# Attention scores from rounded parts in two passes, projections one iteration earlier, row moves split, new orders

## The reference, cut to what matters

```
def _gqa(x, wq, wk, wv, wo):            # 16 heads of 16, 4 key/value heads
    q = (x @ wq.T).reshape(B, S, 16, 16)
    k = (x @ wk.T).reshape(B, S, 4, 16)   # v the same, k and v repeated 4 times
    attn = jnp.einsum('bqhd,bkhd->bhqk', q, k) * scale
    attn = softmax(where(causal, attn, -inf))
    return jnp.einsum('bhqk,bkhd->bqhd', attn, v).reshape(B, S, C) @ wo.T
```

## Time and profile before

| what | us |
|---|---|
| median of 3 runs (2116.47 to 2120.29) | 2118.55 |
| the profiled execution | 2111.37 |
| its span, first to last instruction | 2109.7 |
| busy: TensorE / VectorE / ScalarE / GpSimd | 2036.1 / 1347.3 / 1117.4 / 963.0 |

### The profile page before, as it was taken

How to read it: one execution, slowest core, us unless ns; L and a number is a source line. 1 busy time by engine, 2 the same in 40 slices (tenths; PEclk the granted TensorE clock), 3 DMA queues, 4 the chain that set the end, 5 groups by cost and what they waited for, 6 DMA issues and landing times. The chain is left out here.

```text
span 2109.7 us, 50236 instructions
## 1 busy us (share of the span) xinstructions
PE 2036.1 (97%) x17544; PEld 1752.2 (83%) x17544; DVE 1347.3 (64%) x2818; ACT 1117.4 (53%) x2219; POOL 963.0 (46%) x1062
## 2 busy tenths in 40 slices
PE   7999989999999999989979999999899999999997
PEld 7999985666666666659979999999888888888886
DVE  7888954676777767765636776788654444444452
ACT  6777744666666666655543333344354444454542
POOL 0000002365565556556644444444245656565653
PEclk9999987999999999989989999999999999999998
DMA  8767711133233232229864444544344444545442
GB/s 294 264 260 267 261 59 31 62 104 96 92 108 110 87 106 96 78 92 305 300 218 144 148 151 142 175 150 151 104 96 109 95 111 95 112 96 111 96 83 30
DMA packets 134682, 289.62 MB, mean 137 GB/s; under 512 B 23026, under 2 KB 64755, under 8 KB 128243
## 3 DMA queue, kind: packets, MB, share of 16 engines
q1 hardware_dynamic: 84466, 177.25, 24.9%
q0 software_dynamic: 50048, 110.14, 20.3%
HBM read 187.17 MB, written 95.42 MB: 134 GB/s over the span
## 5 line engine op out<-in xcount | busy, mean ns | idle before, releaser
L1248 DVE TENSOR_REDUCE neg_max<-ring 128x2 f32<-128x512 f32 (+1 forms) x384 | 250.0, 681 | 106.4 <-PE ring L1734 106.1
L1041 POOL TENSOR_SCALAR_AFFINE_SELECT weights_diag<-weights_diag 128x512 f32<-128x512 f32 x256 | 158.3, 643 | 258.4 <-ACT weights_diag L1139 258.1
L2908 POOL DMA_INDIRECT out<-q_t,row_put x128 | 201.8, 1576 | 162.4 <-ACT q_t L2972 137.7
L3046 DVE TENSOR_TENSOR ex_hid<-ex_up_ps,gelu 128x512 f32<-128x512 f32 x128 | 86.9, 688 | 171.8 <-ACT gelu L2956 171.8
L2956 ACT ACTIVATE gelu<-ex_gate_ps 128x512 f32<-128x512 f32 x128 | 76.3, 596 | 187.3 <-PE ex_up_ps L62 187.3
L2379 POOL DMA_INDIRECT picked_rows<-results,lo_row_now x128 | 134.0, 1047 | 56.3 <-issue 29.8
L1139 ACT ACTIVATE weights_diag<-ring 128x512 f32<-128x512 f32 x256 | 138.5, 599 | 24.2 <-PE ring L1752 24.2
L60 PE MATMUL ex_down_ps<-ex_dn_lo,ex_hid_hi 128*128 128x256 f32 x512 | 145.1, 283 | 2.8 <-issue 2.8
L61 PE MATMUL ex_down_ps<-ex_dn_hi,ex_hid_lo 128*128 128x256 f32 x512 | 145.2, 284 | 0.0
L62 PE MATMUL ex_down_ps<-ex_dn_hi,ex_hid_hi 128*128 128x256 f32 x512 | 144.9, 283 | 0.0
L1049 POOL DMA_INDIRECT sorted_rows<-h_sb,row_now x128 | 126.8, 990 | 34.8 <-issue 31.3
(11 more groups left out here) (404 smaller groups left out, 7521.8 us busy)
## 6 DMA issues: line engine op xcount, KB each, us to landing
ug_raw<-in_w_ug SPq DMA_DIRECT2D x32, 1028.0 KB, 5.0
dn_raw<-in_w_dn SPq DMA_DIRECT2D x32, 640.0 KB, 5.2
q_t<-sorted_rows SPq DMA_DIRECT2D x136, 128.0 KB
moe_w<-in_expert_gu SPq DMA_DIRECT2D x16, 1024.0 KB, 4.8
results<-c0n POOLq DMA_DIRECT2D x33, 256.0 KB, 4.4
x_raw<-in_x_t SPq DMA_DIRECT2D x32, 256.0 KB, 5.1
c0n<-c SPq DMA_DIRECT2D x32, 256.0 KB, 4.3
c0r<-c SPq DMA_DIRECT2D x32, 256.0 KB
```

Of the source, the lines that this page charges most:

```text
L1041: nc.gpsimd.affine_select(part, part, [[0, G], [1, P]], ALU.is_ge, 0.0, base=0, channel_multiplier=-1).then_inc(kept_done, 1)
L1248: nc.vector.tensor_reduce(out, src, AX_X, ALU.max, negate=True).then_inc(max_done, 1)
L2908: nc.gpsimd.indirect_dma_start(out=out_rows, out_offset=bass.IndirectOffsetOnAxis(ap=at, axis=0), in_=eo[c][:, n, :], in_offset=None, comp ...
L3046: nc.vector.tensor_tensor(hid[f % 2][:], up_ps[f % 2][:], gelu[f % 2][:], ALU.mult).then_inc(hid_done, 1)
```

## The change

It does the following.

- Queries and keys are kept as rounded parts. `q_t` is [128, 2, 4, 256] fp32r: index 0 the high parts; index 1, for even heads, their low parts in one half of a group's 32 rows and high parts in the other (for odd heads the halves swapped). `k_t` becomes three tiles: the high keys with two rows of ones behind them, and two with high keys in one half of the rows and low keys in the other. The key projection gives the keys twice, in both halves.
- A score is two fp32r matmuls: high by high (16 rows), then both mixed products at once (32 rows). A turned score is one of 512 columns with 18 rows, then two of 256 columns (even and odd heads).
- The maximum is split in two rounded parts (`split_max`), so its transpose has 32 columns and its shift is moved by two DMAs.
- New work: ACT `keep_k` (two activations of 256 columns) and `copy_low` (512); DVE `low_q` (512) and two scalar_tensor_tensor for the keys in place of one tensor_scalar; SP 4 moves (`move_high`) in the iteration of the projection and 8 (`move_beside_low`) in the next, in place of 4.
- Maxima and exponentials take two banks at once (6 instead of 12 of each per sequence).
- Projections are for sequence i+3, square sums for i+4; the loop starts at iteration -2.
- **TensorE's order after:** turned 0, turn_max 0, project_out, scores 0, turn_norm, values 1, turned 1, turn_h, heads 0, scores 1, heads 1, keys_values, turned 2, queries 0 and 1, turn_max 1, scores 2, prefix, gate, turn_out, values 0. In B_ORDER shift_q1 comes before route.
- Buffers of other stages serve as q_t, k_t, and in the expert stage other tiles as `eo`. One wait of SP in the sort (`s == 6`) is dropped.

```diff
@@ turned_scores (PE)
                 for g in range(NKV):
-                    rows = slice(32 * g, 32 * g + HD + 1)
-                    nc.tensor.matmul(slot(2 * r, g)[:], k_t[n][rows, k * P:(k + 1) * P], q_t[n][rows, :, q * P:(q + 1) * P],
-                                     start=True, stop=True).then_inc(turned_done[g], 1)
+                    rows = slice(32 * g, 32 * g + HD + 2)
+                    nc.tensor.matmul(slot(2 * r, g), k_t[n][0][rows, keys], q_t[n][rows, 0, :, toks], start=True, stop=False)
+                for odd in range(2):
+                    for g in range(NKV):
+                        rows = slice(32 * g, 32 * g + HALF)
+                        out = slot(2 * r, g).rearrange("p (j s) -> p j s", j=G)[:, odd:G:2, :]
+                        last = nc.tensor.matmul(out, k_t[n][1 + odd][rows, keys], q_t[n][rows, 1, odd:G:2, toks], start=False, stop=(odd == 1))
@@ scores (PE)
-                    for g in range(NKV):
-                        rows = slice(32 * g, 32 * g + HD)
-                        if r and c == 0 and g >= 2:
-                            until(pe, exp_done, no_more_than(times(12, i, 4 * r + g - 1), 12 * B))
+                    for rest in range(2):
+                        for g in range(NKV):
+                            rows = slice(32 * g, 32 * g + (HALF if rest else HD))
+                            if r and c == 0 and not rest and g == 2:
+                                until(pe, exp_done, no_more_than(times(12, i, 4 * r + 2), 12 * B))
@@ Front
+    def keep_k(self, act, b, k_t):
+        self.nc.scalar.activation(k_t[1], self.piece_b[:, 0:S], ACT.Copy).then_inc(self.k_hi_done, 1)
+        self.nc.scalar.activation(k_t[0], self.piece_b[:, 0:S], ACT.Identity, bias=rows[:, 0:1], scale=rows[:, 1:2]).then_inc(self.k_hi_done, 1)
     def keep_kv(self, dve, b, k_t, v):
-        self.nc.vector.tensor_scalar(k_t[:], self.piece_b[:, 0:S], self.at.one_rows[:], None, ALU.add)
+        dve.wait_ge(self.k_hi_done, 2 * b + 2)
...
+        self.nc.vector.scalar_tensor_tensor(out=k_t[2], in0=high, scalar=rows[:, 3:4], in1=self.piece_b[:, 0:S], op0=ALU.mult, op1=ALU.add).then_inc(self.k_odd_done, 1)
+        dve.wait_ge(self.k_odd_done, b + 1)
+        self.nc.vector.scalar_tensor_tensor(out=k_t[1], in0=high, scalar=rows[:, 2:3], in1=self.piece_b[:, 0:S], op0=ALU.mult, op1=ALU.add).then_inc(self.b_free, 1)
+    def low_q(self, dve, b, q_t):
+        dve.wait_ge(self.q_hi_done, b + 1)
+        self.nc.vector.tensor_tensor(q_t[:, 1, 0:G:2, :], self.piece_a[:].rearrange("p (j s) -> p j s", j=QB), q_t[:, 0, 0:G:2, :].bitcast(F32), ALU.subtract).then_inc(self.a_free, 1)
+    def copy_low(self, act, q_t):
+        self.nc.scalar.activation(q_t[:, 1, 1:G:2, :], q_t[:, 1, 0:G:2, :].bitcast(F32), ACT.Copy).then_inc(self.q_lo_done, 1)
@@ split_max (DVE)
+                dve.wait_ge(max_done, times(12, b, 8 if q else 12))
+                nc.vector.tensor_tensor(max_parts[q][:, 0, :], whole, nothing[:, 0, 0:1].broadcast_to([P, NH]), ALU.add).then_inc(max_hi_done, 1)
+                dve.wait_ge(max_hi_done, times(2, b, 1 if q else 2))
+                nc.vector.tensor_tensor(max_parts[q][:, 1, :], whole, max_parts[q][:, 0, :].bitcast(F32), ALU.subtract).then_inc(max_parts_done[q], 1)
@@ body (SP)
+                if exists(later(i, 2)):
+                    front.move_beside_low(sp, i[1] + 2, q_t[(i[1] + 2) % 4])
                 if exists(later(i, 1)):
                     move_shift(later(i, 1), 1)
-                if exists(later(i, 2)):
-                    move_odd_heads(i)
+                if exists(later(i, 3)):
+                    front.move_high(sp, i[1] + 3, q_t[(i[1] + 3) % 4])
```

302 lines of the change are left out of this document (162 added, 140 removed).

## The result

Slower: 2150.38 us (median of 4 runs, 2146.24 to 2157.73) against 2119.26 (2116.47 to 2120.29) for the kernel before on the same chip, a ratio of 1.0153 with a 95% interval of [1.012, 1.0186]. The prediction was 2100, range 2070 to 2130: wrong in sign and outside the range. The profiled execution after took 2153.45 us with a span of 2151.8, that of before 2111.37 with 2109.7: the two traces differ by 42.1 us, of which the medians show 31.

A forecast was written before the change was run, and what follows sets the result against it. TensorE's own work in program order was taken to bound the attention stage. 28 iterations x (18.6 - 19.43) = -23.2, with +4 and +0.5 giving -18.7: 2092.7 us against the profiled execution, 2100 against the median, range 2070 to 2130.

The forecast's parts named there:

- TensorE's part: Attention stage: shorter turned and score bursts, none gained in round 2, save 2.15 us an iteration, 19.43 becoming 17.28.
- Rival 3: Rounded bursts in row groups bound by their weight loads, over 0.95 us each: slower, 2134 to 2147 us; chance 0.12.
- (a): Queries wait for divide(1), now behind round 1's second-pair reduction: stall 0.35 us in odd iterations, 1.1 in even ones.
- (b): Between gate and turn_out: turn_out waits for the piece keep_logits frees, behind a two-bank reduction of round 2; stall 0.55 us.
- the part on VectorE: VectorE's work grows by net 1.4 to 15.1 us an iteration, binding only by order; with stalls, iterations average 18.6 us.
- stall (c): Score bursts of rounds 1 and 2 wait after two groups for a two-bank exponential: 0.1 us in round 1.
- SP's queue: Moves and shifts fill 11.2 of 18.6 us an iteration; no queue is full, and the shift lands with margin 0.8 at worst.
- rival 4: Shift of the maximum lands late behind eight more moves, 1 us in each iteration: 2120 to 2127 us; chance 0.06.
- Rival 2: VectorE late throughout even iterations (turn_max, out_low, key parts wait), 19.3 us: about 2115 to 2128 us; chance 0.14.
- The sign of being wrong: Listed signs against the forecast: bursts of over 0.9 us, or an iteration under 18.0 or over 19.2 us.
- Start and end: Around the attention loop: first turned score 6.5 us later, 2.5 credited at the end; net +4 us, between 0 and +10.

The follow-up runs named there:

- run 14: Changed kernel with rows to scatter early on VectorE and GpSimd's first pair of scatters between the halves of its triangles: 2118.7 us, ratio 1.0021.
- 5: Changed kernel with VectorE's rows to scatter and four index searches put back ahead of the first maxima of scores round 0: 2153.8 us, ratio 1.0182.
- 7: Run 5 with extra, unread matmuls in two TensorE waits (ahead of the queries; between gate and turned output): 2142.3 us, ratio 1.0123.
- 15: Run 14 with extra, unread matmuls in TensorE's two waits: 2108.2 us, ratio 0.997.
- run 2: Changed kernel with the gate (and prefix) back between the two halves of the queries on TensorE: 2211.3 us, ratio 1.043.
- 9: Changed kernel with exponentials and maxima one bank at a time again, as before the change: 2145.1 us, ratio 1.0129.
- run 12: Run 10 with extra, unread matmuls in two TensorE waits: 2236.4 us, ratio 1.0562.
- 13: Changed kernel without the second pass of the turned scores (8 matmuls fewer in each of three bursts): 2112.1 us, ratio 1.0004.
- 16: Kernel before the change with GpSimd's four scatters of an iteration at the end of its order: 2118.1 us, ratio 1.0024.
- run 18: Run 15 with two instead of three extra matmuls between gate and turned output: 2128.1 us, ratio 1.0055.
- run 1: Changed kernel without the eight moves of rows beside the low parts: 2136.6 us, ratio 1.0089.
- 4: Kernel before the change with eight more moves an iteration, into a tile nothing reads: 2122.0 us, ratio 1.0017.
- 3: Changed kernel with divide(1) put back ahead of the maxima of scores round 1's second half on VectorE: 2163.7 us, ratio 1.021.
- 8: Run 5 with the gate between the turned maxima and scores round 2, logits kept ahead of round 2's maxima: 2156.3 us, ratio 1.0183.
- 10: Changed kernel with GpSimd's four scatters of an iteration at the end of its order: 2235.7 us, ratio 1.0558.

## Why the prediction was wrong

**TensorE's part** held, with one term off. Turned bursts 0.68 us (forecast 0.64), scores of round 0 0.59 (0.54), of round 2 0.95 (0.88). Round 1 takes 0.73 even where nothing waits (run 14, 693.44 to 694.17), and was put at 0.54 like round 0. Savings by these: 3 x 0.39 + 0.38 + 0.24 + 0.05 = 1.84 us instead of 2.15, so 17.6 us of work and not 17.3. VectorE's and ScalarE's work came as forecast too: 363.36 and 321.88 us of 500, 15.1 and 13.3 us an iteration (15.1 and 13.4). Rival 3 did not come: a rounded burst takes 0.59 to 0.95 us. The Trainium skill ("TensorE: Matmul & The Clock Gate", section "The mechanism") states that a load overlaps running matmuls only where the row group differs. With 0.11 us for a load and as much for a stream (an estimate from the earlier trace rows), the score burst of round 0 would then take 4 x 0.22 = 0.88. It takes 0.59, so the trace disagrees.

**Stalls (a) and (b)** came in their place: (b) with 12.0 / 24 = 0.50 us a wait, (a) smaller than forecast, 11.0 us over 24 iterations, 0.46 (0.35 and 1.1, mean 0.7). That (b) agrees with its 0.55 is in part luck: its terms, 0.1 + 1.21 + 0.2 + 0.07, make 1.58, and against 8 x 0.11 = 0.88 they leave 0.70.

**The step that failed** is the sum of an iteration at the end of the part on VectorE: "Odd iterations: 17.2 + 1.0 = 18.2; even: 17.4 + 1.75 = 19.1". An iteration took 20.71 us. The sum took it to be work plus stalls at full clock, so the clock has no term in it, and stall (c), "0.1 in round 1", took the exponential to start as soon as TensorE's burst ends.

First, the clock. The prediction used, with its 1.00, for the time after the change as well, although its own forecast put a microsecond or more of waiting into every iteration of an engine that had none. The granted 0.95 over 500 us is 50 us at the lower level; where TensorE works all through them they cost 25 us, about 1.0 us an iteration. Filling the waits, with TensorE doing more, gave 11.5 us (5 to 7) and 10.5 us (14 to 15), which is net of the filling. That the waits let the clock fall and that this costs time is shown; which waits do it is not. Less idle time went with a lower clock in runs 2 and 9, and the filling of run 12 left it at 0.89.

Second, the late posts: 11.9 us of waits in scores, 0.5 us an iteration where (c) had 0.1, and 2.6 in heads, where the prediction had none; together 0.6 us an iteration. Moving the scatters (with the rows early) gave some 28 us (14), leaving out the second pass of the turned scores some 32 us, 20 of them for its work (13). In both the late posts are gone, but the clock stays at 0.94, so it does not hang on them alone. No row of the kernel before could show the late posts: its bursts don't provoke them, neither with the scatters across a turned score (719.94) nor with the scatters at the end (16). Taking away the scatters' place (14) or the second pass (13) removes them; what holds the posts is not known, and run 18 shows that a condition is missing.

By terms, as an estimate from these rows: 17.6 of work, 1.8 of idle time (42.7 us of 500; of it 0.5 for (a), 0.5 for (b), 0.6 for the late posts) and 1.0 of clock make 20.4 of 20.71 us; 0.3 is not assigned. The same sum gives 17.6 + 0.9 + 1.2 = 19.7 for run 14 (19.67) and 17.6 + 1.8 + 3.9 = 23.3 for run 2 (23.23).

**SP's queue.** "GpSimd's queue has the same transfers" passed over what they run beside. The eight moves cost 14 us in the changed kernel (1), against 4 in the old one (4), where TensorE never waits for anything. In run 1 TensorE is idle for 39.3 us instead of 42.7 and the granted clock is 0.96 instead of 0.95; how the moves bring that about was not followed. The shift landed in time: the turned score of round 0 has no wait for it, so rival 4 did not come.

**No rival** had this case. Rival 3 (2134 to 2147) came nearest in time, by luck, since its loads did not bind. Rival 2 (VectorE late in three places) did not come: `turn_max` and `out_low` kept their margins, until an edit moved them (3, 8). The sign of being wrong that did come was "an iteration ... over 19.2".

**Start and end.** The first turned score starts at 327.29, not 324.8, against 318.37. The once-per-iteration activation runs 32 times from 324.1 to 963.1 (before 314.8 to 927.1): +9.3 us ahead of the loop (forecast 6.5), +26.7 in it, and 42.1 - 36.0 = +6.1 behind it, where 2.5 less were credited. Of the 6.1 us 2.7 lie ahead of the first matmul of the LoRA stage (1142.8 against 1104.1) and 3.5 in that stage, up to the first of the routed experts (1562.8 against 1520.6). That stage takes 417.7 and 419.7 us in the traces of runs 4 and 16, old kernels with the same stage, against 416.5 and 420.0 here, so the 3.5 is no cost of the change that could be told from noise. Without it the price of one more iteration is about +12 and not +4.

## What to carry to other kernels

Where TensorE is busy without a hole, its clock is part of its speed. A change that saves work but brings waits of half a microsecond must be priced at the lower clock too; if the waits can't be removed, check whether filling them costs less. The sum of the waits does not tell the clock: it has to be read from the profile. When an engine starts late, compare the producer's burst with the release and not only the name of the releaser: where a release comes 1 us behind a finished burst, look for what runs beside it. Here the move of another engine's scatters mended it (14). And a kernel tuned by order is a set of margins: two of the old orders put back singly cost some 12 and 59 us.

## What was unexpected of the hardware

- TensorE's releases can arrive over 1 us late, while it goes on issuing: 1.99 us from start to release for a burst of 0.68. This was seen only beside GpSimd's indirect scatters and only in kernels whose turned scores have the second pass. With four scatters in a row (10) VectorE waited 3.19 us, and TensorE stood still for 0.48 and 0.54 us between small matmuls.
- It depends on more than the place of the scatter: 0.87 and 1.42 us at the same distance (15, 18).
- A subtraction of 128x16 on VectorE took 1.23 us instead of 0.18 in run 10, each time beside GpSimd's sum of two 128x512 tiles (1.28 us).
- TensorE's clock fell to the lower of its two levels, again and again, in a stage in which TensorE was busy for 91% and never waited longer than 1.2 us. In run 14 it fell too (0.94), with no wait over 1.1 us; in runs 7, 15 and 18, where two of the waits were filled, it stayed at the upper level (1.00), although run 7 still has its waits for `weights_diag`. Filled in the same places, run 12 was at 0.89. With 38.5 us idle of 500, less than in the changed kernel, run 2 was at 0.83.
